# A post-norm transformer layer on one core: filler matmuls on two 64-row halves of TensorE

## The reference

```python
x = L0_attn_x                                    # (16, 1024, 256)
q, k, v = heads(x @ Wq.T + bq), heads(x @ Wk.T + bk), heads(x @ Wv.T + bv)
attn = softmax(einsum('hbnd,hbmd->hbnm', k, q) / 16)
x = layernorm(x + merge(attn @ v) @ Wo.T + bo)   # no gain, no bias
gate, up = x @ (w_gate / 127).T, x @ (w_up / 127).T      # hidden size 768
x = layernorm(x + (silu(gate) * up) @ (w_down / 127).T)
```

## Time and profile before

| | before |
|---|---|
| median of three runs | 2544.46 us |
| the profiled execution: span | 2544.0 us |
| the profiled execution: granted TensorE clock | 0.990 |
| TensorE, weight loads | 2470.4 us (97%), 884.2 us (35%) |
| ScalarE | 2132.0 us (84%) |
| VectorE | 1399.0 us (55%) |
| GpSimd | 539.6 us (21%) |
| x_pre load, 1024 KB, x17 | 7.3 us from issue to landing |
| x_res load, 1024 KB, x16; store of a half, x32 | 4.8 us; 2.7 us |
| bias add on GpSimd, x16 | 4540 ns each |

### The profile page before, as it was taken

How to read it: one execution, slowest core, us unless ns; L and a number is a source line. 1 busy time by engine, 2 the same in 40 slices (tenths; PEclk the granted TensorE clock), 3 DMA queues, 4 the chain that set the end, 5 groups by cost and what they waited for, 6 DMA issues and landing times. The chain is left out here.

```text
span 2544.0 us, 48910 instructions
## 1 busy us (share of the span) xinstructions
PE 2470.4 (97%) x18062; PEld 884.2 (35%) x18062; DVE 1399.0 (55%) x3008; ACT 2132.0 (84%) x2370; POOL 539.6 (21%) x542
## 2 busy tenths in 40 slices
PE   4999999999999999999999999999999999999996
PEld 2223343433324333343433324333343433333333
DVE  5334556464654655556564654646465565654547
ACT  1997888888888888888888888888889888898881
POOL 2102222131221212222131221212222131221113
PEclk8999999999999999999999999999999999999998
DMA  4112021030212103021021202103121120212000
GB/s 145 50 49 79 28 88 43 23 101 27 91 33 75 59 17 109 23 85 43 31 93 27 93 31 81 55 15 109 27 81 43 37 87 26 93 31 60 27 22 29
DMA packets 81750, 144.20 MB, mean 57 GB/s; under 512 B 27584, under 2 KB 29504, under 8 KB 79424
## 3 DMA queue, kind: packets, MB, share of 16 engines
q1 hardware_dynamic: 79968, 139.81, 17.4%
q10 hardware_dynamic: 1504, 0.66, 0.1%
HBM read 88.48 MB, written 50.33 MB: 55 GB/s over the span
## 5 line engine op out<-in xcount | busy, mean ns | idle before, releaser
L608 ACT ACTIVATE probs<-psum 128x1024 f32<-128x1024 f32 x2048 | 1984.8, 1024 | 312.5 <-PE psum L1045 311.8
L1045 PE MATMUL psum<-probs,v 128*32 128x512 f32 x8192 | 995.7, 600 | 0.9 <-DVE flipped L877 0.4
L1045 PE MATMUL psum<-kstack,qstack 51*128 51x512 f16 x4096 | 637.5, 383 | 18.7 <-ACT probs L608 10.4
L1045 PEld LDWEIGHTS psum<-kstack,qstack 51*128 51x128 f16 x4096 | 150.5, 93 | 679.9 <-ACT probs L608 596.5
L1045 PEld LDWEIGHTS psum<-probs,v 128*32 128x32 f32 x8192 | 211.2, 109 | 470.3 <-issue 468.1
L517 POOL TENSOR_TENSOR ffn<-h,ffn 128x512 f16<-128x512 f32 x192 | 222.0, 1156 | 675.8 <-DVE ffn L793 675.8
L747 DVE SCALAR_TENSOR_TENSOR tanh_out<-tanh_out,psum 128x512 f32<-128x512 f32 x192 | 131.6, 686 | 287.2 <-ACT tanh_out L589 287.2
L510 POOL TENSOR_TENSOR rstd<-vareps,minus_half 128x2 f32<-128x2 f32 x128 | 91.1, 712 | 720.9 <-DVE vareps L815 720.8
L738 DVE SCALAR_TENSOR_TENSOR parts<-psum,scales,parts 128x512 f16<-128x512 f32 x128 | 95.3, 745 | 199.5 <-ACT parts L580 199.4
L1045 PE MATMUL psum<-ffn,gateT 128*128 128x512 f16 x768 | 199.8, 383 | 0.3 <-DVE ffn L781 0.3
L1045 PE MATMUL psum<-ffn,upT 128*128 128x512 f16 x768 | 198.0, 380 | 0.4
(11 more groups left out here) (120 smaller groups left out, 1617.0 us busy)
## 6 DMA issues: line engine op xcount, KB each, us to landing
parts_dram<-parts SPq DMA_DIRECT2D x64, 512.0 KB, 2.9
qstack<-parts_dram SPq DMA_DIRECT2D x384, 64.0 KB, 2.1
kstack<-parts_dram SPq DMA_DIRECT2D x384, 64.0 KB, 2.2
x_pre<-in_x_t SPq DMA_DIRECT2D x17, 1024.0 KB, 7.3
x_res<-in_L_attn_x SPq DMA_DIRECT2D x16, 1024.0 KB, 4.8
out<-x_res SPq DMA_DIRECT2D x32, 512.0 KB, 2.7
kstack<-shift_parts SPq DMA_DIRECT2D x384, 4.0 KB, 1.7
ffn<-in_L_ffn_w_gate SPq DMA_DIRECT2D x1, 768.0 KB, 7.1
```

The lines of the kernel that those rows point to most:

```text
L608: nc.scalar.activation(probs[:, (STEPS * b + k) % SLOTS, 2 * pr:2 * pr + 2, :], scores[pr], ACT.Exp, scale=score_scale[par]).then_inc(prob ...
L1045: return nc.tensor.matmul(o, lhsT, rhs, start=start, stop=stop)
```

## The change

The fillers of the middle batches, apart from x1T and norm, are cut at row 64 (`LOW`, `HIGH`). An item's low-half matmuls run in its own phase, its high-half matmuls in the phase of the item after it, side by side with that item's low half and into another bank. A semaphore `half_made` holds an item's high half until its low half is complete. The last v item is carried into the first phase of the next batch. down's four items become eight `tile` items of one 256-column tile. Each phase is a row of slots, and `VISITS` gives each of 32 periods its slots in three parts: after the odd step's first score pair, after its second, and after the even step's first. So the two score pairs of a step stand apart. x1T and norm items (`SIDES`) go between an even step's second pair and the products. `Rolled` works out the new orders for the other engines; `scale_x` moves to the beginning of the next batch, find_xmax from step 6 to step 9. SP stores and reloads the residual in halves, with the next batch's shift load between them, and issues the stack loads of group 1 ahead of the x load; the bias is added in halves.

```diff
+MAIN = (some("out", 0, 1, 2, 3) + some("qk", *range(8)) + gate_up(*range(2 * HCHUNKS)) + some("tile", *range(TILES))
+        + some("v", 0, 1, 2, 3))
+CARRY = MAIN[-1]
+WIDTH = {"out": 6, "qk": 6, "gate": 4, "up": 4, "tile": 6, "v": 6}
...
+VISITS = [(3, 3, 2), (4, 4, 0), (2, 4, 2), (3, 3, 0), (3, 3, 0), (3, 3, 0), (3, 3, 0), (3, 3, 3), (3, 3, 3), (3, 3, 4),
+          (2, 4, 0), (4, 4, 2), (2, 4, 0), (4, 4, 2), (2, 4, 0), (4, 4, 2), (2, 4, 2), (2, 4, 2), (2, 4, 2), (2, 4, 2),
+          (2, 4, 2), (2, 4, 2),
+          (4, 3, 0), (3, 4, 0), (2, 4, 2), (3, 3, 0), (3, 3, 2), (4, 3, 0), (3, 4, 0), (2, 4, 2), (3, 3, 0), (3, 3, 0)]
+
+SIDES = {3: ("x1T", 0), 4: ("x1T", 1), 5: ("x1T", 2), 6: ("x1T", 3), 12: ("norm", 0), 14: ("norm", 1)}
...
+        slots = []
+        for phase in range(len(MAIN) + (not carries)):
+            low = phase if phase < len(MAIN) else None
+            high = phase - 1 if phase or carried else None
+            wide = [0 if n is None else WIDTH[MAIN[n][0]] for n in (low, high)]
+            slots += [(low if i < wide[0] else None, high if i < wide[1] else None, i) for i in range(max(wide))]
...
+        last = 0.0
+        if carried:
+            last = carry_ready
+            dve = [(last, "v", CARRY[1], -1)] + [(last + 0.3 + 1.5 * hf, "xT", hf, 0) for hf in range(HALVES)]
+        for n in range(done):
+            kind, j = items[n]
+            due = ready[n]
+            if kind in ("qk", "gate"):
+
+                k = act_at[n]
+                self.act[k][1].append((kind, j, n))
+                due = max(due, k + (1.37 if k % 2 else 1.3))
+            last = max(last + 1e-6, due)
+            dve.append((last, kind, j, n))
+            if kind == "qk":
+                pool.append((last + 0.4, kind, j, n))
+            elif kind == "up":
+                pool.append((last + 0.6, kind, j, n))
...
+        for seg in range(SEGMENTS):
+            dve += [(TILES * seg + 1.0, "take", seg - 1, 0), (TILES * seg + 1.4, "scale", seg - 1, 0)]
+        order = lambda entry: entry[0]
+        self.dve, self.pool = sorted(dve, key=order), sorted(pool, key=order)
+
+    def number(self, n):
+        return n if n < 0 else self.place(*MAIN[n])
...
+            def replace_half(b, s):
+
+                store_half(b, s)
+                sp.wait_ge(out_stored, 32 * b + 16 * (s + 1))
+                sp.dma_start(x_res[:, TPH * s:TPH * (s + 1), :], x_v[1:BATCHES][b][:, TPH * s:TPH * (s + 1), :]
+                             ).then_inc(x_res_loaded[s], 16)
 
...
 
             def batch(b, first, last, ahead=2):
-                if first:
-                    load_stack(b, 1)
+                if not first:
+                    sp.wait_ge(scores_ready, UNITS * b)
+                load_stack(b, 1)
                 if not last:
 
                     sp.wait_ge(x_scaled, 2 * b + 4)
                     sp.dma_start(x_pre[:, :, :], xt_v[ahead:BATCHES][b]).then_inc(x_pre_loaded, 16)
-                if not first:
-                    sp.wait_ge(scores_ready, UNITS * b)
-                    load_stack(b, 1)
+                load_shift(b, 1)
+                if not last:
+                    store_parts(b + 1, 0)
                 if not first and not last:
-                    store_parts(b + 1, 0)
...
+                elif last:
+                    replace_half(b - 1, 0)
+                    replace_half(b - 1, 1)
                 else:
-                    store_result(b - 1)
-
-                    sp.wait_ge(out_stored, 32 * b)
-                    sp.dma_start(x_res[:, :, :], x_v[1:BATCHES][b - 1]).then_inc(x_res_loaded, 16)
+                    replace_half(b - 1, 0)
+                    load_shift(b + 1, 0)
+                    replace_half(b - 1, 1)
...
                     find_stats(j)
+                elif kind == "tile":
+                    nc.vector.scalar_tensor_tensor(out=x_res[:, j, :], in0=o[:, 0:DIM], scalar=down_scale[:, 0:1],
+                                                   in1=x_res[:, j, :], op0=ALU.mult, op1=ALU.add).then_inc(ring_free, 1)
+                    if j % 2:
...
                         normalise(j, 1, b - 1, y_ready)
+                    elif n < 0:
+
+                        drain_item(kind, j, n, base(b), b, b - 2, par)
...
 
+            def half_waits(plan, kind, j, n, start, pre, post):
+
+                pe.wait_ge(ring_free, start + n - RINGS + 1)
...
+            def slot(plan, b, low, high, i, w_parts):
+
+                todo = []
+                for rows, which in ((LOW, low), (HIGH, high)):
+                    if which is not None:
+                        kind, j = MAIN[which]
+                        each = COST[kind][0] // WIDTH[kind]
+                        todo += [(m / each, rows, which, kind, j, each * i + m) for m in range(each)]
+                for _, rows, which, kind, j, m in sorted(todo, key=lambda entry: entry[0]):
+                    n = plan.number(which)
+                    if m == 0 and rows is LOW:
+                        half_waits(plan, kind, j, n, base(b), b + 1, b - 1)
+                    elif m == 0:
+                        pe.wait_ge(half_made, len(MAIN) * (b - 1) + which + 1)
+                    ins = half_mm(kind, j, m, rows, bank[RING + (base(b) + n) % RINGS], w_parts)
+                    if m == COST[kind][0] - 1:
+                        ins.then_inc(half_made if rows is LOW else ring_fill, 1)
+
             def stack_here(b, g):
 
                 pe.wait_ge(stack_loaded[g % 2], 16 * LOADS * (2 * b + g // 2 + 1))
...
+            def full(b, par, w_parts):
+
+
+                plan = plan_of(b)
+                for k in range(STEPS):
+                    if k == RELOAD:
+
+                        pe.wait_ge(flag_ready, b + 2)
+                    here = plan.segments[(k - 1) // 2] if k else ((), (), ())
+                    score(b, k, False, (0,))
+                    if k == RELOAD:
+                        pe.reg_load(general, flag[0:1, 0:1])
+                    for low, high, i in here[0 if k % 2 else 2]:
+                        slot(plan, b, low, high, i, w_parts)
+                    score(b, k, False, (1,))
+                    if k % 2:
+                        for low, high, i in here[1]:
+                            slot(plan, b, low, high, i, w_parts)
+                        continue
+                    if k and k // 2 - 1 in SIDES:
+                        n = plan.place(*SIDES[k // 2 - 1])
+                        do_item(plan, n, 0, COST[plan.items[n][0]][0], base(b), b + 1, b - 1, w_parts)
+                    for earlier in (k - 2, k - 1):
+                        if k:
+                            products(b, par, earlier, False)
+                        else:
+                            products(b - 1, 1 - par, STEPS + earlier, False)
+                    if k in plan.unstarted:
+                        g, at = k // PER_GROUP, plan.unstarted[k]
+                        nb = b if g < GROUPS - 1 else b + 1
+                        prepare_shift(GROUPS * b + g + 1, nb, (g + 1) % GROUPS, base(b) + at, base(b) + at - RINGS + 1)
+                for low, high, i in plan.segments[-1][2]:
+                    slot(plan, b, low, high, i, w_parts)
+
             def batch(b, par, first, last, w_parts):
-                plan = PRE_PLAN if first else POST_PLAN if last else FULL_PLAN
+                plan = plan_of(b, first, last)
                 for k in range(STEPS):
                     if k == RELOAD and not last:
 
```

164 lines of the change are left out of this document (125 added, 39 removed).

## The result

The change made the kernel slower: 2656.56 us (median of 4 runs, 2652.37 to 2660.44) against 2544.43 us for the kernel before on the same chip, a ratio of 1.0439 with a 95% interval of 1.0423 to 1.0456. Forecast were 2561 us, 2547 to 2585. The direction was right and the size far too small. The profiled execution has a span of 2657.7 us. The experiments ran on other chips of the same kind, where the kernel before took 2542.6 to 2543.8 us; a difference of 2 or 3 us between a kernel there and the changed kernel here says nothing.

The account below looks back on a forecast made before the run. TensorE bound the kernel before; after the change, waits for exponentials would. 14 x 0.25 us per batch, 13 x 0.9 for the batch-start stall and 0.8 for batch 14 gave +16: 2561 us, range 2547 to 2585.

Parts of the forecast that it names:

- The score chain: From the odd step's first score pair through two exponentials to the even step's second pair: never under 2.42 us.
- plain visits: Two-step periods of TensorE with up to eight filler slots and no transpose or norm: 17 at 4.595 us each.
- a = 4: Three visits with four slots ahead of the odd step's second score pair, which makes that pair late: 4.76 us each.
- transposes: Four visits with a transpose item behind the second score pair, outside the exponentials' cover: 5.185 us each.
- N = 9 and 10: Visits with nine (two) or ten (four) filler slots, where the array's own work decides: 4.77 and 4.99 us.
- All hidden with a visit or more to spare: SyncE's and GpSimd's work, with residual replacement, x load and bias add in halves, was to cost TensorE nothing.
- In gate/up visits ... free: VectorE drains the up item's ring bank before TensorE wants it at 1.95 us into the visit: no wait.
- The stall at the batch's start: VectorE's queue drains x1T0's bank late, so TensorE waits 0.9 us at visit 4; bounds 0 and 3.
- Edges: Batch 1 has no stall at its start, batch 14 gains 0.8 us, batches 0 and 15 keep their work.
- Rival 3: Half waits cost 0.09 us, 1.4 per batch, giving 2580 us; with further bank stalls at the transposes, 24%.
- Rival 2: Exponentials come in time and TensorE's array alone decides, so saved layout changes pay: 2458 us, 4%.
- The rule on weight loads: Loads overlap only matmuls of another row group, so each TensorE slot takes 0.31 us: 2772 us in all, 2%.

Follow-up runs that it names:

- e7: Changed kernel with the moves of e1, e2, e3 and a later maxima search, fillers made whole 128-row matmuls without half waits: 2714.68 us against 2606.75.
- e11: Changed kernel with all-reduce, scalings, scale instructions and transposes moved; then both score pairs put together in every step: 2711.13 us against 2617.35.
- e1: Changed kernel with GpSimd's all-reduce of the row maxima behind four squares, and the scale instructions at place 26, not 22: 2618.66 us.
- e2: Changed kernel with VectorE's scaling of the segments of odd steps 3 and 4 put behind the gate's drain and cut in two: 2628.30 us.
- e15: Changed kernel with the bias added to only 8 of each tile's 256 columns, the rest left out: 2641.89 us.
- e12: Kernel before the change with only the residual stored, loaded and biased in halves: 2564.61 us, ratio 1.0083.
- e17: Changed kernel with the all-reduce behind the fourth square, scale instructions at place 38, and the edits of e2 and e4: 2568.72 us, ratio 1.0099.
- e4: Changed kernel with the x1 transposes ahead of the even step's second score pair, not behind it: 2657.10 us.
- e3: Changed kernel with the four x1 transposes taken at visits 4 to 7, not 3 to 6: 2631.64 us.
- e13: Kernel before with the residual in halves, both bias adds waiting for the second load except in the last batch: 2539.86 us, ratio 0.9985.

## Why the prediction was wrong

- **The score chain** was right: the earlier trace rows gave 2.42, measured 2.42 to 2.43 in every plain visit, whatever its slots; plain visits 4.595, measured 4.60; a = 4: 4.76, measured 4.78; transposes 5.185, measured 5.19; N = 9 and 10: 4.77 and 4.99, measured 4.79 and 5.00. That the six microseconds of layout changes turn into waiting for exponentials is shown; e7 and e11 show both parts of the edit doing their work.
- **The failed step is "All hidden with a visit or more to spare"**, said of SyncE and GpSimd, with the "hidden" of ScalarE beside it. I followed the residual and the x load there, and not the all-reduce, which the same diff had moved from 12.2 to 14.2 and which is GpSimd's longest stretch. It is 3.55 of the 8.3 us of excess (e1). Following it needed one question: which instruction is queued behind it, and who waits for that.
- **"In gate/up visits ... free"** was wrong at four of the twelve gate/up visits. Two of them, 13 and 17, cost 1.95 us (e2). The check used the distance from up to its drain, and not what VectorE's order puts between them where an odd scaling falls into the visit. At visits 12 and 14, 0.57 us together, TensorE waits for the drain of an up item (L903 in the list of waits). Both have a norm item, which takes a number in the ring, so I take that for the cause; no run tested it.
- **The stall at the batch's start** was rightly placed at visit 4, at 0.9 us; measured are 1.32 there and 0.75 at visit 3, where none was foreseen. Half of the 2.07 is the bias add beside VectorE (e15), which the prediction didn't look for: beside it the scaling's multiplication takes 0.96 to 2.1 us and not 0.43.
- **The residual in halves** was "hidden". In the kernel before, it alone costs 21 us (e12); in the changed kernel its two adds cost 15 (e15), at visits 3 and 4. That the trace of before shows no GpSimd add beside a normalise is why it had no price there; it should have been bounded.
- **Edges.** The last batch's gain of 5.6 us was missed. Not all middle batches of the kernel before have the same length, as the prediction says: batch 1 has 154.9 us and not 152.05.
- **Rivals.** Rival 3 named further bank stalls with too small a price, and its half wait cost nothing in this kernel. Rival 2 fell with the plain visits of 4.60 us. The rule on weight loads, by which slots would be some 0.3 apart, fell too: they are 0.22 apart, and the measurement decides.

With the stalls of visits 9, 10, 13 and 17 cured the kernel stands at 2569 us (e17), near the forecast of 2561 and still slower than before. Part of that nearness is luck. e17 also has e4's edit, which the forecast's kernel has not, and which gives 0.30 us at each of visits 5 and 6: some 8 us in 14 batches, by an estimate from the table. Without it about 2577 would be left. The sum was that of a kernel without these stalls and with a shorter one at the batch's start.

## What to carry to other kernels

When a diff changes the order on one engine, follow every item of that order to what is queued behind it and to who waits for that, also for the engines that are 20% busy. Measure by place (here the length of each visit) and not by the total: e3's total agreed with a forecast whose reasons were wrong, and e4's showed nothing of the gain at its visits 5 and 6. Splitting a transfer lets its consumer start earlier, and the earlier place can be the dearer one: e13 has the halves and starts late.

## What the runs showed of the hardware

- A GpSimd two-input operation held up VectorE's SBUF-to-SBUF operations until it had ended: 2.75 us for two normalisations that take 0.74 (e12), 1.10 for a multiplication that takes 0.43 (after). Beside e13's adds of 4.69 us a VectorE operation that reads PSUM kept its 0.75.
- The all-reduce of one column held GpSimd from 1036.7 to 1050.15, 13.5 us, of which the profile shows 0.38 as busy; in the other middle batches of this kernel it was 13.2 to 14.9.
- An idle stretch of 1.67 us of TensorE was followed by some 3 us at the lower granted clock; behind 3 of the 14 stalls of this kind no such stretch shows.
- Half matmuls on the two row halves start together and follow 0.22 us apart, weight loads included (after, visit 18); a change between the 64-row and the 128-row layout costs 0.10 us (e7: 0.32 for 0.22).
